# A weight load moved to mid-step, ScalarE's high parts moved to the third unit, three VectorE operations moved by one split

## The reference

```python
xn = _layernorm(x, axis=-1)
x = x + _L0_attn_ref(xn, Wq, Wk, Wv, Wo, We) + _L0_ffn_ref(xn, gate_w, w1, b1, w2, b2)
```

## Time and profile before

| | us |
|---|---|
| median of 3 runs | 727.4 |
| lowest and highest | 726.87, 727.62 |
| the profiled execution | 725.8 |
| its span | 724.1 |

### The profile page before, as it was taken

The page is one execution under the profiler, slowest core; times in us unless marked ns, Lnnn a source line. Parts: engine busy times, 40 slices in busy tenths (PEclk is TensorE's granted clock), DMA queues, the critical chain, the costliest instruction groups (busy, mean ns, idle before and its releaser), DMA issues.

```text
span 724.1 us, 25378 instructions
## 1 busy us (share of the span) xinstructions
PE 663.7 (92%) x8084; PEld 448.1 (62%) x8084; DVE 650.1 (90%) x1177; ACT 531.9 (73%) x1123; POOL 514.5 (71%) x613
## 2 busy tenths in 40 slices
PE   0377899999999999799999999999999999999996
PEld 0263445555555555599999999999455555555554
DVE  8989989999999999699999999999899999898991
ACT  2593388888888888667767767777787787787885
POOL 8680477777677656077777887787688888888782
PEclk9986799999999999999999999999999999999999
DMA  8859466776676676633333333332577777877652
GB/s 249 307 170 336 135 166 169 182 200 161 175 209 173 174 191 174 160 76 96 93 96 93 97 96 90 97 92 75 142 155 179 191 178 183 173 178 187 176 122 67
DMA packets 124919, 113.37 MB, mean 157 GB/s; under 512 B 16416, under 2 KB 112416, under 8 KB 124832
## 3 DMA queue, kind: packets, MB, share of 16 engines
q1 hardware_dynamic: 115600, 90.63, 47.7%
q0 software_dynamic: 8192, 16.86, 9.6%
q10 hardware_dynamic: 1040, 4.76, 1.8%
HBM read 64.72 MB, written 47.19 MB: 155 GB/s over the span
## 4 chain that ended last, share of the span: by engine, by line
PE 65%; DVE 13%; SPq 8%; DMA 6%; issue 5%; ACT 2%; ACTq 0%; DVEq 0%
PE bank L1266 13%; PE mx L1255 13%; PE bank L1135 12%; PE bank L1113 11%; PE mx L1147 7%; DVE mx L961 6%; DMA stack<-qk_dram 6%; PE bank L1033 2%; PE bank L1247 2%; PE bank L1195 2%; DVE A L796 2%; SPq L331 2%; PE bank L1157 1%; ACT A L715 1%; PE bank L1164 1%
## 5 line engine op out<-in xcount | busy, mean ns | idle before, releaser
L715 ACT ACTIVATE A<-bank 128x512 f32<-128x512 f32 x502 | 278.2, 597 | 63.8 <-PE bank L1135 55.8
L961 DVE TENSOR_REDUCE mx<-mx 128x4 f16<-128x1024 f32 x256 | 302.7, 1205 | 19.1 <-PE mx L1147 14.7
L1135 PE MATMUL bank<-stack 113*128 113x256 f16 x1004 | 170.4, 276 | 1.3 <-ACT A L715 0.8
L761 ACT ACTIVATE rows<-mx,b 128x256 f32<-128x256 f32 x284 | 120.1, 480 | 57.7 <-PE mx L1255 55.3
L556 POOL DMA_INDIRECT slots_x<-rows,pos x128 | 123.6, 966 | 51.8 <-PE bank L1135 32.0
L570 POOL TENSOR_SCALAR rows<-rows,slot_p 128x128 f32<-128x128 f32 x142 | 124.6, 887 | 43.9 <-DVE rows L1009 43.9
L607 POOL DMA_INDIRECT rows<-slots_y,pos x128 | 121.5, 950 | 37.5 <-issue 17.3
L1113 PE MATMUL bank<-A,V 128*32 128x256 f32 x2048 | 137.9, 387 | 1.7 <-ACT A L715 1.6
L1135 PEld LDWEIGHTS bank<-stack 113*128 113x128 f16 x1004 | 72.4, 97 | 89.4 <-ACT A L715 53.8
L1266 PE MATMUL bank<-w,rows 128*128 x1704 | 107.7, 219 | 0.6 <-DVE rows L1003 0.6
L1003 DVE TENSOR_TENSOR rows<-rows 128x512 f16<-128x512 f32 x142 | 101.4, 714 | 4.9
(11 more groups left out here) (145 smaller groups left out, 684.9 us busy)
## 6 DMA issues: line engine op xcount, KB each, us to landing
stack<-ctx_rest SPq DMA_DIRECT2D x64, 256.0 KB
stack<-qk_dram SPq DMA_DIRECT2D x128, 96.0 KB
rows<-slots_x SPq DMA_DIRECT2D x71, 129.0 KB, 2.3
slots_y<-rows SPq DMA_DIRECT2D x71, 128.0 KB, 1.8
qk_dram<-hi_qk SPq DMA_DIRECT2D x64, 128.0 KB
stack<-ctx_high SPq DMA_DIRECT2D x128, 64.0 KB
slots_x<-A ACTq DMA_DIRECT2D x1, 4644.0 KB, 20.3
w_stage<-in_w SPq DMA_DIRECT2D x8, 512.0 KB
```

Of the source, the lines that this page charges most:

```text
L715: act.activation(A[:, n % NA, :, :].rearrange("p h s -> p (h s)"), scores(k, n)[:, :], ACT.Exp, scale=SCALE).then_inc(s_xp, 1)
L761: act.activation(h32[r % 2][:, fc, :], bank[fc][:, 0:SLOT], ACT.Gelu_apprx_tanh, bias=b1[:, bass.ds(e + fc, 1)], scale=1 / FS).then_inc(s_ ...
L961: dve.tensor_reduce(mx[:, a, 8 * qt:8 * qt + 8].rearrange("q (i e w) -> q i e w", i=2, e=2)[:, :, g % 2], MX[u % 2][:, :].rearrange("q (i ...
L1135: mm = pe.matmul(scores(k, n)[:, i * S:(i + 1) * S], stack[0:SHIFT + 1, par, h, 1, c * P:(c + 1) * P], stack[0:SHIFT + 1, par, h, 0, :], s ...
```

## The change

There are three edits. In SyncE's step the load of w_stage (L407) moves from the end of the step into the pass g = 0 of the loop over head halves, after the write of Q and K and ahead of the pass g = 1; its wait for s_wlo goes with it. ScalarE's high part (L741) moves from unit 6 to unit 2, except in step 1. In the prologue VectorE does project_lo(1), context_lo(0) and context_lo(1) after the splits 10, 9 and 13 in place of 9, 8 and 12.

```diff
--- before.py
+++ after.py
@@ -400,11 +400,11 @@
                             for h in range(2):
                                 sp.wait_ge(s_st[par3][h], n_st)
                         write(par3, n_hq, n_lq)
-                c = low_chunk(s, k, first_half)
-                if c is not None:
-                    sp.wait_ge(s_wlo, 2 * c + 2)
-                    src = W12[:, (c + 1) * WCH:(c + 2) * WCH] if isinstance(c, int) else W12[:, bass.ds((c + 1) * WCH, WCH)]
-                    sp.dma_start(w_stage[:, :], src).then_inc(s_wst, 16)
+                    c = low_chunk(s, k, first_half)
+                    if g == 0 and c is not None:
+                        sp.wait_ge(s_wlo, 2 * c + 2)
+                        src = W12[:, (c + 1) * WCH:(c + 2) * WCH] if isinstance(c, int) else W12[:, bass.ds((c + 1) * WCH, WCH)]
+                        sp.dma_start(w_stage[:, :], src).then_inc(s_wst, 16)
 
             attention_steps(sp, 0, attend)
 
@@ -735,7 +735,7 @@
                     if k == 1 and u == 6:
                         act.wait_ge(s_routed, 2)
                         act.wait_ge(s_place, 2)
-                    if u == 6 and ch is not None:
+                    if u == (6 if k == 1 else 2) and ch is not None:
                         act.wait_ge(s_wst, 16 * (ch + 1))
                         dst = w12[:, 0, ch * WCH:(ch + 1) * WCH] if isinstance(ch, int) else w12[:, 0, bass.ds(ch * WCH, WCH)]
                         act.activation(dst, w_stage[:, :], ACT.Copy, scale=FS).then_inc(s_whi, 1)
@@ -887,10 +887,10 @@
             scale(2)
             for g in range(4, NG):
                 split(g)
-                if g in (5, 9):
-                    project_lo((g - 5) // 4)
-                if g in (8, 12):
-                    context_lo((g - 8) // 4)
+                if g in (5, 10):
+                    project_lo(g // 10)
+                if g in (9, 13):
+                    context_lo((g - 9) // 4)
             route(0)
             context_lo(2)
             route(1)
```

## The result

| us | before | after |
|---|---|---|
| median of 6 runs each | 727.13 | 738.99 |
| lowest and highest | 726.2, 728.4 | 735.84, 740.52 |
| the profiled execution | 725.8 | 735.88 |
| its span | 724.1 | 734.1 |

The changed kernel is slower: the ratio of the times over all runs is 1.0153, with an interval of 1.0126 to 1.018.

A forecast was written before the change was run, and what follows sets the result against it. TensorE, busy 92% of the span, bounds the kernel. Waits of 10.8 us, less 2.3 and 0.45 from ScalarE, plus 0.1 in the prologue, make it 8.1 slower: 733.9 profiled, 735.5 as median; range 727.0 to 740.

The forecast's parts named there:

- marks set for it: Signs in the changed profile: L407 before L327, L1147 of unit 4 waiting 0.5 to 2 us (step 15: 3), even steps 13.2.
- C: Rival: DMA engines take w_stage beside the half-1 load, no push; 1.5 us faster, 725.9 us; chance 0.12.
- push: Delay of the half-1 stack load by w_stage's 512 KB ahead on SyncE's queue: 1.9 us, bounds none and 2.3.
- D: Rival: TensorE's waits come out at the size of the gains, push 0.2 to 0.9 us; 727.4 us; chance 0.12.
- The wait, step by step: TensorE at L1147 of unit 4, seven odd steps: later issue plus push minus slack, 10.8 us in all.
- issue of L327 later: SyncE issues the half-1 load later, waiting for GpSimd's low parts: 0.6 to 1.9 us, 2.9 in step 14.
- the slack: Time between the half-1 load's landing, 5.1 us after issue, and TensorE's need of it: 1.5 to 1.9 us.
- a push of 2.3: Upper bound of the half-1 load's delay behind w_stage, in us; it set the range's upper end, 740.
- ScalarE's gain: L741 in unit 2 lets L1195 come earlier: 0.38 us in each of steps 3 to 13, 2.3 in all.
- The tail gain: Step 15: ScalarE's last exponentials end earlier without L741 ahead of them; gain 0.45 us, bounds 0 and 1.06.
- The prologue: VectorE's three operations one split later: SyncE's issuing, which ends the prologue, starts 0.1 us later; bounds -0.4 and 0.5.
- Rival A: GpSimd's standstill does not come back, step 15 waits 0.8 us; sum 5.8, time 733.2 us; chance 0.22.

The follow-up runs named there:

- e12: Only the load of w_stage moved to mid-step, against the kernel before, third chip: 735.74 against 725.66 us, ratio 1.0125.
- e11: The changed kernel with the mid-step load cut to 64 of 1024 columns, third chip: 724.24 against 725.66 us for the kernel before, ratio 0.9991.
- e10: Only ScalarE's high part moved, unit 6 to unit 4 (not in step 1), against the kernel before, third chip: 725.88 against 725.66 us, ratio 0.9997.
- e9: The whole change unaltered, run again on the second chip against the kernel before: 736.23 against 724.86 us, ratio 1.0135.
- e6: The changed kernel with GpSimd's two low parts earlier, first chip: 823.25 against 809.25 us for the kernel before, ratio 1.0159.

## Why the prediction was right in direction and short in size

**The mechanism holds.** Three of the marks set for it are there: L407 between L346 and L327, L1147 of unit 4 late in the odd steps, even steps of 13.21. The waits of step 3 (2.43) and step 15 (4.02) are longer than the 0.5 to 2 and the 3 that it named. e12 shows that the load's move alone makes the loss, and e11 that the loss goes when the load shrinks. The point from which C would have decided, a push under 0.6 us, was not reached in any step. Nor were D's 0.2 to 0.9.

**The wait, step by step.** How much later L1147 of unit 4 starts than before, counted from the mark:

| step | 3 | 5 | 7 | 9 | 11 | 13 | 15 | sum |
|---|---|---|---|---|---|---|---|---|
| predicted | 1.0 | 1.55 | 1.55 | 1.55 | 1.0 | 1.0 | 3.1 | 10.8 |
| measured | 2.5 | 0.5 | 0.9 | 1.2 | 0.5 | 0.9 | 4.1 | 10.6 |

With the 0.44 for shift rows in step 3 it is 11.0. That the sum came out so near is luck: the errors of single steps, up to 1.5, cancel. Two of its three terms, in the even step before each:

| step | 2 | 4 | 6 | 8 | 10 | 12 | 14 |
|---|---|---|---|---|---|---|---|
| issue of L327 later, predicted | 0.6 | 1.2 | 1.6 | 1.9 | 0.6 | 0.6 | 2.9 |
| measured | 1.1 | 1.1 | 1.5 | 1.6 | 0.6 | 0.5 | 3.0 |
| push, predicted | 1.9 | 1.9 | 1.9 | 1.9 | 1.9 | 1.9 | 1.9 |
| measured | 2.7 | 1.3 | 1.4 | 1.6 | 1.8 | 1.6 | 2.8 |

(The push is the time from the issue of L327 to the start of L1147, 6.43 to 7.85 us, less the 5.1 that the prediction had for before. That 5.1 was an estimate; the 5.15 of e11 in step 15 bears it out. The third term, the slack, follows from the same 5.1 and was 1.2 to 1.9.) The issue was sized well from the rows of GpSimd and SyncE. The push was right in its mean, 1.9, and wrong as a constant: 1.3 to 2.8. The value of 2.3 taken as its upper bound was passed in two steps. Of the two, step 14 is the one that e11 shows by itself (2.70). In step 2 even the small load of e11 left TensorE 0.81 of wait. SyncE was held up there: its two issues of L331 behind the small load took 1.84 us, where they took 0.86 before. What held them up was not separated. The Trainium skill's size, bytes over 436 GB/s from the page "DMA: Bandwidth & Descriptors", section "Anatomy of one DMA — SWDGE (gpsimd) path", gave 1.2. The page has it for DMAs that GpSimd issues; these are SyncE's. The least of the seven, 1.3 and 1.4, come near it, the mean and the two that cost most do not.

**The range.** It ended at 740, "a push of 2.3". By the prediction's own terms that push gives waits of 3 x 1.4 + 3 x 1.95 + 3.5 = 13.55 and, less 2.65, a time of 738.3. The measured median of 738.99 lies above that: it was inside the range by a margin that no term of the sum stood for.

**The step that failed: the clock.** The sum priced a wait of TensorE at its own length. After the waits of 2.43 and 4.02 us the products that followed ran at half clock for 3.4 us each. What it cost can be read from what comes behind L1147. In step 3 the way from it to the next mark is 11.17 after and 137.66 - 128.03 = 9.63 before; adding ScalarE's gain of 0.38 and taking off the shift rows' 0.44 leaves 1.5. In step 15 the way to the first L1266 is 316.23 - 298.24 = 17.99 and was 305.21 - 288.36 = 16.85, so 1.1. Together 2.6 us, a quarter of the loss. The same way takes 16.61 in e11 and 16.49 in e12, both at full clock, so the 1.1 may be up to 1.5. In the kernel before, e10 and e11 the granted clock is 1.00 from 105 to 306 us: the fall comes with the long waits. This was not in the prediction, though the trace of the kernel before could have raised the question: between 60 and 80 us, where TensorE works for 14.6 us of 20, its granted clock is 0.74.

**ScalarE's gain.** 0.38 in each of six steps was right; e11 shows it without cover. The tail gain of 0.45 was wrong. TensorE's last wait for exponentials is 1.03 after and 1.17 before, 1.22 in e11, which has L741 in unit 2, and 1.11 in e12, which has it in unit 6, both at full clock. So L741 is not what the wait is for; ScalarE is late there with it or without it. The failed step is "Without L741 ahead of them they would end 0.45 earlier".

**The prologue.** 0.1 was forecast. The mark of step 2 is at 110.50 after and 110.85 before, but at 110.71, 109.82, 109.64 and 110.00 in e9, e11, e10 and e12, of which the last two have no edit in the prologue. So this mark moves by 1 us between executions, and no effect can be read from it. The 0.35 here goes with another difference: between 80 and 105 us TensorE is granted 0.86 before and 0.93 after. Where the forecast was made, at the first L1147 after the prologue, it is 79.68 before and 79.81 after, 0.1 later as forecast; but e9 to e12 have it anywhere from 78.95 to 79.77, so this agreement shows little.

**The sum, remade.** 11.0 of waits, 2.6 of clock, less 2.3 of ScalarE and 0.35 at the mark of step 2: 10.95. The first L1266 comes 316.23 - 305.21 = 11.0 later. The rest of the kernel was 1.0 shorter in this pair, which gives the 10.0 between the spans. The forecast of 8.1 lacked the clock (2.6) and had the tail (0.45) too much. The median is 3.1 above the profiled execution and not the 1.6 of before: the six runs spread over 4.7 us where those of before spread over 2.2. e9 suggests why, with a longer wait and 13.6 us at low clock in all. For the other runs there is no trace, only the mean granted clock: 0.978 and 0.980 in the two of 736 us, 0.970 to 0.976 in the four of 739 to 741. That fits and does not prove it.

**Rival A.** GpSimd's standstill came back before the same scatter, the 114th of 128, in every trace of the comparison and of e9 to e12: 5.57 before, 5.38 after, 5.29, 5.02 and 5.57 in e9, e10 and e12, and 3.45 in e11. So A fell. The load is not its cause, as it stands in the kernel before and in e10 with the load in its old place. What is the cause stays open.

**What stays open.** Why engines pause together on the first chip, and why e6 is slower there. Whether another queue for w_stage, or a place behind the second stack half, would keep ScalarE's 2.3 us: neither was run. In e10 and e11 nothing was faster than the kernel before by more than the measurement can tell.

## What to carry to other kernels

Before a large load is moved ahead of a small one on the same queue, work out the small one's slack to its reader, and hold against it the large one's traffic as well as whatever its wait delays. A wait of TensorE of some 2 us at a stretch can cost more than itself, since the work around it may be granted half the clock; put that in the range. And the gain of a move belongs to the place where the engine idles: the same operation in unit 4 gained nothing, in unit 2 0.38 a step.

## What the runs showed of the hardware

- The length of a wait alone did not tell whether the clock would fall. It fell around waits of 1.92 (e12, step 3), 2.43 (after, step 3), 3.65 and 4.59 (e9), and 4.02 us (after, step 15). It stayed full after 3.40 in step 15 of e12, and after 1.92 in step 9 of e9, the very length after which it had fallen in e12. The two rows at full clock, of e12, in which L1113 takes its usual 1.07:

```profile
298.07 0.61 PE L1147 MATMUL mx<-stack 64*128 64x256 f16 x8 [3.40 <-DMA stack<-qk_dram]
...
299.15 1.07 PE L1113 MATMUL bank<-A,V 128*32 128x256 f32 x16
```

  Nor did it fall at one fixed distance: 1.5 us after the end of the wait in step 3 of the changed kernel (131.7 against 130.17), and 1.3 us ahead of it in e9 (130.3 against 131.65). After the waits of 1.2 us or less in these steps it stayed full. Each stretch at the lower level lasted 3.4 or 6.8 us. By the Trainium skill ("TensorE: Matmul & The Clock Gate", section "HAM oscillation — how this bites in real kernels") a wait for a DMA can leave the products behind it at the lower clock. Five of the seven waits above agree and two do not; the price of 3.4 us at the lower level, 1.1 and 1.5 us a time, is from the rows alone.
- One program, the kernel before, took 725 us on two chips and 809 us on another; an effect of 1.25% on one of the first could not be seen on the other. What is to be compared has to run on the chip on which the difference is.
